# Rounds of four decays, one pool of PSUM banks, and convolution taps that read PSUM, in a fused decoder layer on one core

## The chip, the cores and the metric

The kernel runs on one core of a Trainium2 chip, in fp32 with bf16 and fp16 in places. The metric is the device time of one launch in microseconds. Engines are named as in the profile: PE is TensorE, DVE is VectorE, ACT is ScalarE, POOL is GpSimd, SP is the queue that issues most DMAs.

## What is computed

One decoder layer on 8 batches of 256 tokens of 512 channels: x gains a state-space mixer, then cross-attention to a context, then a mixture of 8 experts (top 2). The change touches the mixer alone. Cut to what matters, per batch:

```
zxbcdt = layernorm(x) @ W_in.T            # z 1024, xBC 1280, dt 64 channels
xBC = silu(causal_conv(xBC, conv_w))      # 4 taps over the tokens, per channel
dt  = softplus(dt_raw + dt_bias);  cum = cumsum(dt * A) within chunks of 128 tokens
L   = exp(cum_i - cum_j) for j <= i       # 64 heads, each 128 x 128 per chunk
Y   = ((C B^T) * L * dt) @ xs  +  exp(cum) * C @ S_prev  +  D * xs
y   = Y * silu(z);  x = x + rmsnorm(y) @ W_out.T
```

## The kernel before

The work is cut into pieces. `mixer_slots` and `attention_slots` give every piece a slot, `whole_order` sorts them, and each engine walks the one list and issues the pieces that are its own; semaphores carry what a piece needs from another engine. So each engine works strictly in this order, and TensorE runs ahead of the others until a semaphore holds it.

The mixer has 256 slots, 32 to a batch, 16 to a chunk, 8 to a unit (a batch, a chunk, half of the heads). A slot s stands for 4 heads and goes through five pieces:

- `decay` (PE, L626): a matmul over 60 rows of bf16 makes the differences of cum for 4 heads, 128x512, in one PSUM bank. Even slots use array rows 0 to 63, odd ones 64 to 127, and two decays are issued together in every even slot.
- `bound` (ACT, L732) takes them out of PSUM into decay, `exp` (ACT, L736) exponentiates in place, two slots after the decay.
- `mix_g` (POOL) for even and `mix_v` (DVE) for odd slots (both L741): the product with C B^T, three slots after, into mix.
- `heads` (PE, L638): for two slots at once, six slots after the decay, 8 products of 32 output columns each (16 records in the trace), into the bank y of the unit.

Around them lie the projections (`x`, `z`, `dt`, L544; each x or z piece has 4 matmuls, 8 records), the turns (L549, L576), the states (L593), the expansion of exp(cum) to channels (`expand`, L598, on 32 rows), the carried part (`carry`, L604), the sum of squares (`ones`, L608) and the output projection (`out`, L616). The table of the expansion is a constant of 64x512, loaded at the start among ten constant loads.

The convolution of a pair of channel tiles: ACT copies the bank of the projection to raw (L690), with three zero columns ahead of it, and once more, scaled with the last tap, to conv (L692, two pieces); DVE adds the other three taps for each of the two tiles (`taps`, L825, 128x256 each, three in a row with a wait between); ACT takes tanh (L700) and DVE gates (L833). The bank is free after ACT's copy.

PSUM has 8 banks. Three (decay_ps) serve decays and later the attention's scores; five (work_ps) serve all the rest. `shared_banks` hands them out in the order of the list: a new piece gets the bank whose last reader stands earliest in the list, and TensorE waits for that reader. Five decay and five mix tiles rotate in SBUF.

Of the kernel before, what the change touches and what calls it, by code (L numbers as in the profile page):

```python
# [40 lines left out]
PAIRS = [4, 0, 1, 2, 3]  # L41
ITEMS = [(kh, par, t, quad) for kh in range(2) for par in range(2) for t in range(TPB) for quad in range(4)]
# [22 lines left out]
class Steps:  # L65
# [5 lines left out]
    def settle(self, instruction):  # L71
        self.n += 1
        instruction.then_inc(self.sem, 1)
        self.e.wait_ge(self.sem, self.n)
# [10 lines left out]
def mixer_slots():  # L85
# [6 lines left out]
    for i in range(NS_STEPS + 6):  # L92
        for s, stage in ((i - 6, "heads"), (i - 3, "mix"), (i - 2, "exp")):
            if 0 <= s < NS_STEPS and (stage != "heads" or s % 2):
                put(i, ((stage + ("_v" if s % 2 else "_g")) if stage == "mix" else stage, s))
        if i < NS_STEPS:
            if i % 2 == 0:
                put(i, ("decay", i), ("decay", i + 1))
            put(i, ("bound", i))

    for u, (b, c, hf) in enumerate(UNITS):
        v = NHALF * u
        if hf == 0:
            put(v - 1, ("cb", b, c))
            put(v, ("cb_mask", b, c))
# [16 lines left out]
        put(f + 12, ("rstat", b, c, hf))  # L122
# [14 lines left out]
    for b in range(NB):  # L137
# [21 lines left out]
        for j, at in zip(PAIRS, (13, 17, 20, 24, 29)):  # L159
# [7 lines left out]
        for j, at in enumerate((32, 36, 39, 43)):  # L167
            put(r + at, ("z", b, j, 0))
            put(r + at + 1, ("z", b, j, 1))
            put(r + at + 2, ("z_tanh", b, j))  # L170
            put(r + at + 3, ("z_gate", b, j))
# [23 lines left out]
def shared_banks(order, size, use):  # L195
# [11 lines left out]
    return bank, opened_after  # L207

# [115 lines left out]
def layer_kernel(nc, A, out):  # L324
# [11 lines left out]
    with ExitStack() as top:  # L336
# [39 lines left out]
        with ExitStack() as st:  # L376
            work_ps = [bank(st, f"work_ps{i}") for i in range(5)]
            decay_ps = [bank(st, f"decay_ps{i}") for i in range(3)]
# [3 lines left out]
            w_in = sb(st, "w_in", [P, KD, 2 * HID + 2 * NS + NH])  # L382
            xnT.append(sb(st, "xnT1", [P, KD, L]))
            raw = [sb(st, f"raw{i}", [P, 2, L + TAPS - 1]) for i in range(2)]
# [1381 lines left out]
```

## Time and profile before

| | us |
|---|---|
| median of 3 runs (1450.73 to 1457.11) | 1454.51 |
| span of the profiled execution (the profile gives no other time of it) | 1459.2 |
| PE busy / DVE / ACT / POOL | 1351.0 / 875.7 / 722.8 / 584.9 |
| PE busy from 700 to 800, 800 to 900, 900 to 1000 us (attention) | 86.9, 83.7, 86.0 |
| PE busy from 1100 to 1459 us (experts) | 348.4 |

The mixer lies between some 51 and 670 us, attention overlaps its end and goes on to about 1000 us, and the experts fill the rest. Busy time counts an engine as busy from the start to the end of its instructions; ends of matmuls are modelled, so that the distance between starts says more than a duration. In a timeline, one line is a run of like instructions: the start, how long the run lasts, and in brackets how long the engine had stood before it and what released it.

### The profile page before, as it was taken

The page shows a single profiled execution, that of the slowest core. Times are in us where ns is not written, and L with a number is a line of the kernel's source. Part 1 is how long each engine was busy: PE and PEld are TensorE (multiplying, and loading weights), DVE is VectorE, ACT ScalarE, POOL GpSimd, SP SyncE. Part 2 cuts the span into 40 slices and gives each one's busy share as a digit, 9 for nine tenths or more (in the row PEclk, how much of TensorE's full clock was granted, in tenths as well). Part 3 has the DMA queues.
Part 4 walks back from the last instruction along what each step waited for, and adds up shares of the span by engine and source line. Part 5 has one row for each costly group of instructions (what it writes and reads, how often), then busy time and mean ns, then how long its engine had stood idle before and what let it go on. Part 6 is the DMA issues. An engine that isn't in the chain of part 4 may idle for free.

```text
span 1459.2 us, 23236 instructions
## 1 busy us (share of the span) xinstructions
PE 1351.0 (93%) x7783; PEld 740.9 (51%) x7783; DVE 875.7 (60%) x1838; ACT 722.8 (50%) x1390; POOL 584.9 (40%) x871
## 2 busy tenths in 40 slices
PE   6799999999999999998888888888999999999997
PEld 4456566566656665654343433324444444444443
DVE  5797888979797879757888898755111111111111
ACT  2677657667667676663587766672111111111110
POOL 1365455555555465674223246143222222222221
PEclk9899999999999999997899999898999999999999
DMA  9000000000000000000211110002343354244322
GB/s 338 10 8 5 8 5 1 12 1 12 1 8 5 8 5 8 13 1 4 98 34 35 34 34 31 30 30 74 119 135 113 70 136 138 45 130 131 58 44 29
DMA packets 40292, 73.02 MB, mean 50 GB/s; under 512 B 18544, under 2 KB 22896, under 8 KB 39152
## 3 DMA queue, kind: packets, MB, share of 16 engines
q1 hardware_dynamic: 30240, 48.10, 9.4%
q0 software_dynamic: 8736, 20.61, 7.7%
q10 hardware_dynamic: 1200, 2.82, 0.5%
q8 instruction: 66, 1.08, 0.3%
q14 instruction: 50, 0.41, 0.1%
HBM read 148.91 MB, written 19.99 MB: 116 GB/s over the span
## 4 chain that ended last, share of the span: by engine, by line
PE 70%; DVE 18%; issue 4%; ACT 3%; POOL 2%; DMA 1%; SPq 1%; POOLq 0%; DVEq 0%; ACTq 0%
PE work_ps L544 13%; PE gate_ps L1540 9%; PE up_ps L1540 9%; PE down_ps L1524 9%; PE work_ps L616 7%; DVE conv L825 6%; PE work_ps L549 4%; PE work_ps L638 3%; DVE maxes L1230 3%; PE work_ps L1056 3%; PE mturn_ps L549 2%; PE decay_ps L626 2%; PE decay_ps L1047 2%; DVE mix L741 1%; PE work_ps L1073 1%
## 5 line engine op out<-in xcount | busy, mean ns | idle before, releaser
L544 PE MATMUL work_ps<-xnT,w_in 128*128 128x256 f32 (+1 forms) x1216 | 303.8, 395 | 0.8 <-ACT xnT L650 0.8
L741 POOL TENSOR_TENSOR mix<-decay,cbm 128x512 f32<-128x512 f32 x128 | 182.0, 1423 | 223.8 <-ACT decay L736 193.4
L544 PEld LDWEIGHTS work_ps<-xnT,w_in 128*128 128x128 f32 (+1 forms) x1216 | 221.8, 190 | 64.3 <-issue 34.0
L732 ACT ACTIVATE decay<-decay_ps 128x512 f32<-128x512 f32 x256 | 154.2, 603 | 117.1 <-PE decay_ps L626 116.4
L1628 POOL DMA_INDIRECT out_dram<-y_out,ids x39 | 61.9, 1587 | 334.5 <-DVE row_w L1592 230.7
L1230 DVE TENSOR_REDUCE maxes<-work_ps 128x2 f32<-128x512 f32 x256 | 166.2, 683 | 32.4 <-PE work_ps L1032 31.1
L825 DVE SCALAR_TENSOR_TENSOR conv<-raw,conv_w,conv 128x256 f32<-128x256 f32 x240 | 179.1, 752 | 7.0 <-ACT conv L692 1.3
L1128 ACT ACTIVATE prob<-decay_ps 128x512 f32<-128x512 f32 x256 | 142.3, 609 | 72.8 <-PE decay_ps L1047 71.9
L1607 DVE TENSOR_TENSOR act<-gelu,up_ps 128x512 f32<-128x512 f32 x39 | 26.8, 688 | 252.1 <-PE up_ps L1540 252.1
L736 ACT ACTIVATE decay<-decay 128x512 f32<-128x512 f32 x256 | 164.1, 641 | 4.6 <-PE work_ps L544 3.0
L1540 PE MATMUL gate_ps<-w_e,xgT 128*128 x312 | 140.5, 593 | 1.4 <-ACT xgT L1557 1.0
L1524 PE MATMUL down_ps<-w_e,actT 128*128 x312 | 140.4, 593 | 0.8 <-ACT actT L1570 0.8
L1540 PE MATMUL up_ps<-w_e,xgT 128*128 x312 | 140.3, 592 | 0.0
L616 PE MATMUL work_ps<-w_out,yz 128*128 128x512 f32 x256 | 132.0, 640 | 4.7 <-DVE yz L883 4.1
L741 DVE TENSOR_TENSOR mix<-decay,cbm 128x512 f32<-128x512 f32 x128 | 100.4, 785 | 35.0 <-PE work_ps L638 19.3
L1599 DVE TENSOR_SCALAR y_out<-down_ps,row_w 128x512 f32<-128x512 f32 x39 | 29.3, 751 | 122.3 <-PE down_ps L1524 122.3
L1032 PE MATMUL work_ps<-kT,qT 48*128 48x256 f16 x512 | 92.4, 295 | 6.5 <-DVE maxes L1230 2.0
L1540 PEld LDWEIGHTS up_ps<-w_e,xgT 128*128 128x128 f32 x312 | 59.3, 190 | 74.6 <-issue 74.6
L1047 PE MATMUL decay_ps<-qT,kT 49*128 49x512 f16 x256 | 90.5, 412 | 6.7 <-ACT prob L1128 5.4
L638 PE MATMUL work_ps<-mix,xdt 128*32 128x128 f32 x2048 | 83.8, 282 | 8.5 <-DVE mix L741 7.7
L1557 ACT ACTIVATE xgT<-mturn_ps 128x512 f32<-128x512 f32 x39 | 23.3, 597 | 136.7 <-PE mturn_ps L549 136.7
L1570 ACT ACTIVATE actT<-mturn_ps 128x512 f32<-128x512 f32 x39 | 23.3, 597 | 128.4 <-PE mturn_ps L549 128.4
(270 smaller groups left out, 1990.0 us busy)
## 6 DMA issues: line engine op xcount, KB each, us to landing
w_e<-c_experts_dram SPq DMA_DIRECT2D x39, 3072.0 KB
normed_tokens<-r_xn SPq DMA_DIRECT2D x17, 256.0 KB, 2.1
out_dram<-x_sb SPq DMA_DIRECT2D x17, 256.0 KB, 2.5
x_sb<-x_dram SPq DMA_DIRECT2D x1, 3072.0 KB, 16.8
w_in<-c_w_inT_dram ACTq DMA_DIRECT2D x1, 2560.0 KB, 12.3
w_in<-c_w_inT_dram SPq DMA_DIRECT2D x1, 2048.0 KB, 9.1
w_out<-c_w_outT_dram SPq DMA_DIRECT2D x1, 2048.0 KB, 22.2
RT<-cum_scratch SPq DMA_DIRECT2D x32, 48.0 KB
```

The costliest lines, as they stand in the source:

```text
L544: m = e.matmul(ps[0:width, at:at + L], w_in[:, k, col:col + width], xnT[b % 2][:, k, :], start=(k == 0), stop=(k == KD - 1))
L616: m = e.matmul(work(stage, tile)[:, :], yz[tile % 2][:, ct, :], w_out[:, ct, :], start=(ct == 0), stop=(ct == NCZ - 1))
L638: m = e.matmul(work("y", b, c, hf)[32 * quad:32 * quad + 32, ct * P:(ct + 1) * P], xdt[hf][:, 2 * HG * ct + h, :], mix[(s - 1 + h // HG) % ...
L732: e.activation(decay[s % 5][:, :], decay_ps[s % 3][:, :], ACT.Relu, scale=-1.0).then_inc(piece_done[stage], 1)
L736: e.activation(decay[s % 5][:, :], decay[s % 5][:, :], ACT.Exp, scale=-1.0).then_inc(piece_done[stage], 1)
L741: return e.tensor_tensor(four(mix[s % 5]), four(decay[s % 5]), cb, ALU.mult)
L825: m = e.scalar_tensor_tensor(o, raw[n % 2][:, i, k:k + L], conv_w[:, c, k:k + 1], o, ALU.mult, ALU.add)
L1047: e.matmul(score_ps[s % 3][:, :], kT[b % 3][base:base + PARTS + 1, k, t * P:(t + 1) * P], qT[b % 3][base:base + PARTS + 1, 2 * k:2 * k + 2 ...
L1128: e.activation(prob[s % 12][:, :], score_ps[s % 3][:, :], ACT.Exp, scale=DH ** -0.5).then_inc(piece_done[stage], 1)
L1230: e.reduce_max(maxes[b % 2][:, t, first:first + 2], work("max", b, p)[:, :].rearrange("p (h t) -> p h t", h=2), AX.X).then_inc(piece_done[ ...
L1524: m = e.matmul(down_ps[i % 2][:, :], actT[i % 2][:, k, :], w_e[:, bass.ds(place[i], 1), k, 2 * EH:].rearrange("p o n -> p (o n)"), start=( ...
L1540: m = e.matmul(ps[:, :], xgT[i % 2][:, k, :], w_e[:, bass.ds(place[i], 1), k, off:off + EH].rearrange("p o n -> p (o n)"), start=(k == 0), ...
```

## The change

- `decay`: four at once, at the head of every fourth slot. `heads` for the two pairs of the round before come directly ahead of them, 8 slots after their own decays. `bound` takes two decays in the first slot of the round and two in the second; `exp` and the products keep their slots.
- The eight banks become one pool, from which mixer pieces take any, attention's pieces the first five, and scores the last three as before. Decays take part in it. Some pieces move by a slot or less, among them `cb`, `cb_mask`, `carry`, `carried`, `rstat`, `z_gate`, and the projections.
- The product is written in place into the decay tile; ten decay tiles replace five decay and five mix tiles.
- The taps read the projection in PSUM; the copy to raw is gone. `taps` is issued as two pieces of three, in which the two tiles alternate. The bank is held until the second of them.
- `dt` (from the second batch), `dt_turn` and `expand` work on all 128 rows and columns: their tiles get 128 partitions, with zeros in the lower half, and the constant of the expansion becomes 128x1024.

```diff
-    for i in range(NS_STEPS + 6):
-        for s, stage in ((i - 6, "heads"), (i - 3, "mix"), (i - 2, "exp")):
-            if 0 <= s < NS_STEPS and (stage != "heads" or s % 2):
-                put(i, ((stage + ("_v" if s % 2 else "_g")) if stage == "mix" else stage, s))
-        if i < NS_STEPS:
-            if i % 2 == 0:
-                put(i, ("decay", i), ("decay", i + 1))
-            put(i, ("bound", i))
+    for i in range(NS_STEPS + 2 * GROUP):
+        if i % GROUP == 0:
+            for s in range(i - 2 * GROUP + 1, i - GROUP, 2):
+                if s >= 0:
+                    put(i, ("heads", s))
+            for s in range(i, min(i + GROUP, NS_STEPS)):
+                put(i, ("decay", s))
+        if 0 <= i - 3 < NS_STEPS:
+            put(i, ("mix_v" if (i - 3) % 2 else "mix_g", i - 3))
+        if 0 <= i - 2 < NS_STEPS:
+            put(i, ("exp", i - 2))
+        for s in range(NS_STEPS):
+            if i == s - s % GROUP + s % GROUP // 2:
+                put(i, ("bound", s))
...
-            put(v - 1, ("cb", b, c))
-            put(v, ("cb_mask", b, c))
+            put(v - 2, ("cb", b, c))
+            put(v - 1, ("cb_mask", b, c))
...
-            put(f + 3, ("carry", b, c, hf))
-            put(f + 5, ("carried", b, c, hf), ("dx_add", b, c, hf))
+            put(f + 2, ("carry", b, c, hf))
+            put(f + 3, ("carried", b, c, hf), ("dx_add", b, c, hf))
...
-        for j, at in zip(PAIRS, (13, 17, 20, 24, 29)):
+        for j, at in zip(PAIRS, (13, 17, 21, 25, 29)):
...
-        for j, at in enumerate((32, 36, 39, 43)):
+        for j, at in enumerate((33, 37, 41, 45)):
...
-        return (stage, *key[:2]), ("x_copy" if stage == "x" else "z_gate", *key[:2])
+        return (stage, *key[:2]), ("taps", *key[:2], 1) if stage == "x" else ("z_gate", *key[:2])
...
+    if stage == "decay":
+        return ("decay", *key), ("bound", *key)
+    if stage == "score":
+        return ("score", *key), ("exponent", *key)
...
-            k = min(range(size), key=lambda i: -1 if last[i] is None else at[last[i]])
+            k = min(allowed(*piece), key=lambda i: -1 if last[i] is None else at[last[i]])
...
+def banks_for(mixer):
+
+    def allowed(stage, *key):
+        if stage == "score":
+            return [5 + key[0] % 3]
+        return range(BANKS if stage in mixer else 5)
+
+    return allowed
...
-            expand = sb(st, "expand", [NH, NCZ // 2, P])
+            expand = sb(st, "expand", [P, NCZ, P])
...
-                channels(e, work(*piece), 0, b, HID + CONV, NH).then_inc(piece_done[stage], 1)
+                channels(e, work(*piece), 0, b, DT_COL, P if b else NH).then_inc(piece_done[stage], 1)
...
-                if s % 2 == 0 and s >= 2:
-                    e.wait_ge(*done("bound", s - 2))
...
-                e.activation(raw[n % 2][:, :, TAPS - 1:TAPS - 1 + L], ps[:, :].rearrange("p (c t) -> p c t", c=2), ACT.Copy)
...
-                if s >= 5:
-                    e.wait_ge(*done(*mixed(s - 5)))
-                e.activation(decay[s % 5][:, :], decay_ps[s % 3][:, :], ACT.Relu, scale=-1.0).then_inc(piece_done[stage], 1)
+                if s >= NDECAY:
+                    e.wait_ge(*done("heads", s - NDECAY + 1 - s % 2))
+                e.activation(decay[s % NDECAY][:, :], work("decay", s)[:, :], ACT.Relu, scale=-1.0).then_inc(piece_done[stage], 1)
...
+        def tap(e, b, j, i, late):
+            o = conv[(5 * b + PAIRS.index(j)) % 2][:, i, late:]
+            return e.scalar_tensor_tensor(o, work("x", b, j)[:, i * L:(i + 1) * L - late], conv_w[:, 2 * j + i, TAPS - 1 - late:TAPS - late], o, ALU.mult, ALU.add)
...
-                for k in range(TAPS - 1):
-                    m = e.scalar_tensor_tensor(o, raw[n % 2][:, i, k:k + L], conv_w[:, c, k:k + 1], o, ALU.mult, ALU.add)
-                    if k < TAPS - 2:
-                        own.settle(m)
-                m.then_inc(piece_done[stage], 1)
+                if part == 0:
+                    e.wait_ge(*done("x_copy", b, j))
+                    first = own.mark(tap(e, b, j, 0, 1))
+                    own.mark(tap(e, b, j, 1, 1))
+                    own.wait(first)
+                    tap(e, b, j, 0, 2).then_inc(piece_done[stage], 1)
+                else:
+                    own.wait(own.n)
+                    second = own.mark(tap(e, b, j, 1, 2))
+                    e.wait_ge(*done("taps", b, j, 0))
+                    own.mark(tap(e, b, j, 0, 3))
+                    own.wait(second)
+                    tap(e, b, j, 1, 3).then_inc(piece_done[stage], 1)
```

## Rows read from the trace of the kernel before

**Rows 1.** Busy time by stretches: start:end, length, busy us of each engine, PEclk, DMA.
```profile
136.00:636.00 500.00, 484.86 (x3420) 310.65 (x3418) 406.47 (x689) 337.77 (x674) 276.21 (x374) 0.99 0.03 6
323.00:350.00 27.00, 24.78 (x192) 16.03 (x191) 26.36 (x40) 18.81 (x40) 13.82 (x12) 1.00 0.05 10
350.00:402.00 52.00, 52.00 (x360) 33.52 (x360) 39.09 (x69) 35.40 (x70) 28.93 (x43) 1.00 0.02 4
...
183.00:189.00 6.00, 6.00 (x20) 4.44 (x21) 5.93 (x8) 2.19 (x6) 3.86 (x4) 0.62 0.01 1
```

**Rows 2.** Chain of waits, 322 to 350 us: start, us, what.
```profile
324.56 1.50 DVE conv L825
...
347.01 0.50 DVE conv L825
```

**Rows 3.** Timeline of TensorE, 335 to 350 us and at 493 us.
```profile
335.41 0.28 PE L576 MATMUL work_ps<-ident,dtT 64*128 64x64 f32 x2
...
336.84 0.39 PE L626 MATMUL decay_ps<-RT,LT 60*128 60x512 bf16 x2 [0.51 <-ACT decay L732]
...
339.79 0.64 PE L638 MATMUL work_ps<-mix,xdt 128*32 128x128 f32 x16 [0.64 <-DVE mix L741]
341.11 1.96 PE L616 MATMUL work_ps<-w_out,yz 128*128 128x512 f32 x4 [0.68 <-DVE yz L883]
...
493.18 0.28 PE L576 MATMUL work_ps<-ident,dtT 64*128 64x64 f32 x2
```

**Rows 4.** Timeline of TensorE, three stretches: starts of neighbouring groups.
```profile
276.67 1.99 PE L544 MATMUL work_ps<-xnT,w_in 128*128 128x256 f32 x8
278.50 0.60 PE L549 MATMUL work_ps<-ident,xn 128*128 128x128 f32 x4
279.03 0.39 PE L626 MATMUL decay_ps<-RT,LT 60*128 60x512 bf16 x2
279.35 1.99 PE L544 MATMUL work_ps<-xnT,w_in 128*128 128x256 f32 x8
281.27 0.64 PE L638 MATMUL work_ps<-mix,xdt 128*32 128x128 f32 x16
...
288.92 0.66 PE L549 MATMUL work_ps<-ident,xbc 128*128 128x128 f32 x4
...
403.97 1.89 PE L544 MATMUL work_ps<-xnT,w_in 128*128 128x256 f32 x8
405.79 0.39 PE L626 MATMUL decay_ps<-RT,LT 60*128 60x512 bf16 x2
```

**Rows 5.** Timeline of TensorE in the attention, 802 us.
```profile
802.16 0.39 PE L1047 MATMUL decay_ps<-qT,kT 49*128 49x512 f16 x1
802.16 0.39 PE L1032 MATMUL work_ps<-kT,qT 48*128 48x256 f16 x2
```

**Rows 6.** Lines of VectorE one by one: durations in ns, least/median/most.
```profile
L825 DVE SCALAR_TENSOR_TENSOR conv<-raw,conv_w,conv x240: 468/485/1560, 29.3 to 608.4; 128x256 f32<-128x256 f32 x120
...
L838 DVE SCALAR_TENSOR_TENSOR zs<-zs,work_ps x32: 665/682/689, 58.2 to 636.5; 128x512 f32<-128x512 f32 x32
...
L865 DVE TENSOR_TENSOR xdt<-work_ps,dt_tok x64: 403/410/425, 57.0 to 659.1; 128x256 f32<-128x256 f32 x64
...
L883 DVE TENSOR_TENSOR yz<-yz,zs x32: 691/693/1049, 80.5 to 685.3; 128x512 f32<-128x512 f32 x32
...
L900 DVE SCALAR_TENSOR_TENSOR x_sb<-work_ps,rstats,x_sb x16: 735/745/752, 118.4 to 703.4; 128x512 f32<-128x512 f32 x16
```

**Rows 7.** Busy time by stretches, line L825 alone.
```profile
323.00:350.00 27.00, 14.81 (x18) 1.00 0.05 10
```

**Rows 8.** Timeline of ScalarE in the first batch.
```profile
44.35 0.58 ACT L690 ACTIVATE raw<-work_ps 128x512 f32<-128x512 f32 x1
```

**Rows 9.** DMA issues: count, size, median us to landing.
```profile
xbc<-c_select_dram SPq DMA_DIRECT2D x1, 512.0 KB, 4.7
...
expand<-c_expand_dram SPq DMA_DIRECT2D x1, 128.0 KB, 4.3
```

More of the change, by code:

```diff
@@ L121, in mixer_slots @@
         put(f + 11, ("ones", b, c, hf))
-        put(f + 12, ("rstat", b, c, hf))
+        put(f + 11.5, ("rstat", b, c, hf))
         if hf == 1:
@@ L170, in mixer_slots @@
             put(r + at + 2, ("z_tanh", b, j))
-            put(r + at + 3, ("z_gate", b, j))
+            put(r + at + 2.9, ("z_gate", b, j))
     return slots
@@ L376, in layer_kernel @@
         with ExitStack() as st:
-            work_ps = [bank(st, f"work_ps{i}") for i in range(5)]
-            decay_ps = [bank(st, f"decay_ps{i}") for i in range(3)]
+            work_ps = [bank(st, f"work_ps{i}") for i in range(BANKS)]
             w_out = sb(st, "w_out", [P, NCZ, DIM])
@@ L381, in layer_kernel @@
             xw = sb(st, "xw", [P, NH, HP])
-            w_in = sb(st, "w_in", [P, KD, 2 * HID + 2 * NS + NH])
+            w_in = sb(st, "w_in", [P, KD, X_COL + CONV])
             xnT.append(sb(st, "xnT1", [P, KD, L]))
-            raw = [sb(st, f"raw{i}", [P, 2, L + TAPS - 1]) for i in range(2)]
             conv = [sb(st, f"conv{i}", [P, 2, L]) for i in range(2)]
@@ L404, in layer_kernel @@
             wdec_tok = [sb(st, f"wdec_tok{i}", [P, NH]) for i in range(2)]
-            ecum = [sb(st, f"ecum{i}", [NH, P]) for i in range(2)]
+            ecum = [sb(st, f"ecum{i}", [P, P]) for i in range(2)]
             LT = sb(st, "LT", [P, TPB, NG // 2, P], BF16)
@@ L411, in layer_kernel @@
             state = sb(st, "state", [P, HID])
-            decay = [sb(st, f"decay{i}", [P, HG * P]) for i in range(5)]
-            mix = [sb(st, f"mix{i}", [P, HG * P]) for i in range(5)]
+            decay = [sb(st, f"decay{i}", [P, HG * P]) for i in range(NDECAY)]
             eexp = sb(st, "eexp", [P, 512])
@@ L568, in tensor_mixer @@
                     e.wait_ge(load_w["xbc" if stage == "x" else "z"], 16)
-                col = (HID if stage == "x" else 0) + (2 * j + half) * P
+                col = (X_COL if stage == "x" else 0) + (2 * j + half) * P
                 channels(e, work(stage, b, j), half * L, b, col, P).then_inc(piece_done[stage], 1)
@@ L597, in tensor_mixer @@
                 for k in range(4):
-                    m = e.matmul(work(*piece)[:, k * P:(k + 1) * P], expand[heads_of(hf), k, :], ecum[b % 2][heads_of(hf), :], start=True, stop=True)
+                    m = e.matmul(work(*piece)[:, k * P:(k + 1) * P], expand[:, 4 * hf + k, :], ecum[b % 2][:, :], start=True, stop=True)
                 m.then_inc(piece_done[stage], 1)
@@ L622, in tensor_mixer @@
                     e.wait_ge(load_cum[c], 16 * 8 * (b + 1))
-                if s % 2 == 0 and s >= 2:
-                    e.wait_ge(*done("bound", s - 2))
                 rows = slice(64 * (s % 2), 64 * (s % 2) + DROWS)
-                e.matmul(decay_ps[s % 3][:, :], LT[rows, c, (hf * NHALF + s % NHALF) // 2, :], RT[rows, c, :], start=True, stop=True).then_inc(piece_done[stage], 1)
+                e.matmul(work(*piece)[:, :], LT[rows, c, (hf * NHALF + s % NHALF) // 2, :], RT[rows, c, :], start=True, stop=True).then_inc(piece_done[stage], 1)
             elif stage == "heads":
@@ L638, in tensor_mixer @@
                         m = e.matmul(work("y", b, c, hf)[32 * quad:32 * quad + 32, ct * P:(ct + 1) * P], xdt[hf][:, 2 * HG * ct + h, :],
-                                     mix[(s - 1 + h // HG) % 5][:, h % HG * P:(h % HG + 1) * P], start=(odd == 0), stop=(odd == 1), tile_position=(0, 32 * quad))
+                                     decay[(s - 1 + h // HG) % NDECAY][:, h % HG * P:(h % HG + 1) * P], start=(odd == 0), stop=(odd == 1), tile_position=(0, 32 * quad))
                 m.then_inc(piece_done[stage], 1)
@@ L740, in mixing @@
             four = lambda a: a[:, :].rearrange("p (h i) -> p h i", h=HG)
-            return e.tensor_tensor(four(mix[s % 5]), four(decay[s % 5]), cb, ALU.mult)
+            return e.tensor_tensor(four(decay[s % NDECAY]), four(decay[s % NDECAY]), cb, ALU.mult)
+        def tap(e, b, j, i, late):
+            o = conv[(5 * b + PAIRS.index(j)) % 2][:, i, late:]
+            return e.scalar_tensor_tensor(o, work("x", b, j)[:, i * L:(i + 1) * L - late], conv_w[:, 2 * j + i, TAPS - 1 - late:TAPS - late], o, ALU.mult, ALU.add)
         def vector_mixer(e, own, piece):
@@ L767, in vector_mixer @@
                 for i in range(2):
-                    e.memset(raw[i][:, :, 0:TAPS - 1], 0.0)
                     e.memset(xdt[i][:, :, :], 0.0)
+                    e.memset(ecum[i][NH:, :], 0.0)
+                e.memset(dtT_all[NH:, 5, :], 0.0)
+                e.memset(wdecT_all[NH:, :], 0.0)
                 e.wait_ge(load_ident, 16)
```

55 lines of the change are left out of this document (29 added, 26 removed).

## The prediction

> **What bounds the kernel now.** The change touches only the mixer, some 51 to 670 us, so I began with the busy time by stretches [rows 1]. Over 136 to 636 us TensorE is busy 484.9 of 500 us, VectorE 406.5, ScalarE 337.8, GpSimd 276.2. Batches repeat: the decay turn at 335.41 comes again at 493.18, two batches on [rows 3], so one batch takes 78.9 us. Inside one batch there are two regimes [rows 1]. From 350 to 402 TensorE is busy for all 52 us and VectorE for 39.1. From 323 to 350 VectorE is busy 26.4 of 27 us and TensorE 24.8. The chain of waits, read next, agrees: its links from 324.56 to 347.01 are nearly all VectorE's, mostly the convolution's taps (L825) [rows 2], and TensorE's timeline shows it standing for 0.51, 0.64 and 0.68 us there, for a decay's reader, a product and yz [rows 3]. So TensorE and VectorE each decide in a part; ScalarE and GpSimd do not.
>
> **TensorE's busy time is not all work.** It runs in modes: full array, heads on 32 columns (L638), decays on 64 rows (L626), the expansion on 32 rows. Starts of neighbouring groups give what a change of mode costs [rows 4]. The same eight L544 matmuls take 1.83 us with heads before and full work behind (276.67 to 278.50), 1.82 with full work before and decays behind (403.97 to 405.79), and 1.92 with decays before and heads behind (279.35 to 281.27). So a change behind a group costs 1.92 - 1.83 = 0.09 us, and a full group that follows a tiled one is 1.92 - 1.82 = 0.10 longer. The second differs by group: four L549 take 0.66 after decays and 0.60 after full work, 0.06 more. Over the mix of groups I take 0.07; 0 and 0.10 are its bounds.
>
> **The change, part by part.**
>
> 1. Rounds of four. Now every two slots have one run of heads and one of decays, in different slots: 128 runs each, 512 changes in or out. 39 neighbouring pairs save one each; the expansion and the two dt stages bring it to 504 in the written order, 224 of them into full work. With the rounds the order is full, heads, decays, full once in four slots: 64 x 3 = 192, and 3 for the first batch's dt: 195, 66 of them into full work. The later dt, dt_turn and expand become full work. Gone: (504 - 195) x 0.093 = 28.7 us, and (224 - 66) x 0.07 = 11.1: together 39.8 us, 5.0 us a batch (bounds 28.7 and 44.5). It is all on the path where TensorE decides.
> Four decays in a row don't occur in the trace. If the second pair's weights could not be loaded beneath the first, each round would lose 0.09: 5.8 us. The nearest rows are in the same 64-row mode: two L1032 of one row group with 256 columns each take 0.39 us, and so does one L1047 with 512 [rows 5], which leaves nothing for weights. I take 0; the 5.8 stays in the range.
> The Trainium skill, "TensorE: Matmul & The Clock Gate", Part 3, The mechanism, lets a weight load pass under a running matmul only where the row group differs. By it the gain would be those 5.8 us smaller; the rows speak against it.
>
> 2. The taps. There are 240, at least 468 ns, 485 in the median, 1560 at most [rows 6]. Another operation that reads two SBUF tiles stretches as well (L883, 691 to 1049), while those with an operand in PSUM don't: L838 665 to 689, L865 403 to 425, L900 735 to 752 [rows 6]. So I put the stretching down to GpSimd at work on SBUF beside it, and it should go with the operand. The tap will read PSUM and one SBUF tile and take a scalar per partition, as L900 does: 745 ns for 512 columns, less 682 - 410 = 272 for half the columns (L838, L865): 473, and I take 480. Bounds: 410, and what it costs now. In the VectorE stretch lie 18 taps with 14.8 us [rows 7], 823 ns each: 18 x 0.48 = 8.6, so 6.2 us go. There VectorE would need 26.4 - 6.2 = 20.2 us, and TensorE 24.8 - 27/79 x 5.0 = 23.1. TensorE becomes the bound there too. The 27 - 24.8 = 2.2 us of standing go in each of 8 batches: 17.6 us.
> The Trainium skill, "VectorE: DVE Perf Modes", The TRN2 errata, gives an operation that reads PSUM 62 cycles more than one from SBUF, some 65 ns as an estimate from it. Here the least of L883 (SBUF) is 691 and the median of L838 (PSUM) 682 [rows 6], so no such term. By the page a tap would be dearer by it: 1.2 us in a VectorE stretch, 9.4 us in all if VectorE still decided there, none if not.
>
> 3. ScalarE loses the copy to raw: 40 x 0.58 = 23 us [rows 8], off the path in the steady part. The product in place (L741) costs what it did.
>
> 4. New waits. Eight banks are shared, and a round takes four at once. By the order, seven of a batch's 32 decays get a bank whose reader stands only one slot ahead (x_add, yz, xdt, carried), and the heads of slot 4g+3 have two slots after their product in place of three. TensorE is in order, so behind a waiting decay stands everything, the projections that feed VectorE too. In the TensorE stretch VectorE has 12.9 of 52 us free; in the other it would have 23.1 - 20.2 = 2.9. I take 1 us of new standing a batch: +8 us; bounds 0 and 3 a batch, the upper one a little over what stands today.
>
> 5. Start. The first batch's chain of convolution pairs runs through ScalarE's copy to raw; 44.35 is the last of three [rows 8]: -1.7 us. The expansion table grows from 128 to 512 KB, ahead of the last constants: 128 KB landed in 4.3 us, the 512 KB of select in 4.7 [rows 9]: +0.4, and under 2. Four new memsets of at most 256 columns cost under the 0.41 of L865 each: +0.6, between 0 and 1.6.
>
> 6. dt_turn moves 128 columns for 64; an L549 of 128 columns is some 0.11 us (0.53 from 278.50 to 279.03, less 0.09, by four) [rows 4], so 3 x 0.05 x 8 = 1.2 us. dt with 128 output columns streams the same 256. No DMA is added beyond the table; SP's cum_in waits for the 16th decay of a half, now issued two slots earlier, and nothing else passes it.
>
> Sum: -39.8 - 17.6 + 8 - 1.7 + 0.4 + 0.6 + 1.2 = -48.9 us on the profiled execution's span of 1459.2, the only time that the profile gives for it. The span is 4.7 us above the median of 1454.5, so I take the difference off the median: 1405.6, or 1405. Attention and the experts (from 700 us) should not move.
>
> **The rivals.**
>
> A. The waits that leave also give back clock. From 183 to 189 us the granted clock is 0.62 [rows 1], the lower level of 1.2 GHz for some three quarters of it, though TensorE is busy throughout; those 6 us hold the work of 3.7, so 2.3 are lost. If no new waits come (-8) and two such places go (-5): 1392. For: VectorE has 2.9 us spare. Against: shorter leads, and that the clock over the whole stretch is 0.99, so such places are few.
>
> B. The short leads bite in VectorE's stretch: three rounds lie there and each stands 1 us, 16 us over the sum: 1421. For: VectorE's chain is unbroken for 23 us there. Against: 6 us are taken from it.
>
> C. The taps don't become short, since what stretches them is not the second SBUF operand but the tile they write. VectorE then needs its 26.4 us as now, the stretch stays at 27 us, and only 52/79 of the 39.8 comes: -26, and +1 for the start: 1430. Against: the PSUM rows [rows 6]. It is also the case in which the change of the convolution does not do what it says.
>
> D. Slower: the round as a lockstep. Each of 64 rounds begins with heads that need the last product, and its fourth decay needs a bank just read; ScalarE gets four decays at once and none between, and TensorE stands in each round until ScalarE and VectorE have caught up. It decides from 48.9/64 = 0.76 us a round on. At 1.0 us, one and a half of VectorE's operations (0.68), it gives +15: 1469. Against: in 52 of 79 us VectorE is 75% busy, and a round has some 9 us of other matmuls.
>
> **How the numbers follow.** Forecast 0.52, A 0.15, B 0.19, C 0.07, D 0.07. The likeliest is 1405, its own range 1392 to 1418. From A's 1392 the upper bound of part 1 (-5) and an easier start (-4) lead to 1383; above, C ends at 1430, and D is left out. A difference within 0.5% (7.3 us) is what a measurement of this kernel can't tell from none. Slower by more: D, 0.06; same: 0.03, D's milder end and what lies between C and it; faster: the rest, 0.91.
>
> **What would show it.** L638 and the decays together in the timeline, once in four slots. A batch of 72 to 74 us. Taps of 450 to 500 ns without spread (part 2); over 550 is C. TensorE busy over 97% in the former VectorE stretch; standing in front of decays or heads there is B, in every round D. From the first of four decays to the full group behind them 0.55 us (part 1); 0.64 means that the second pair's weights are not hidden. The forecast is wrong if the batch comes out above 76 us, or if the stages from 700 us on change their length.

## The result, and the profile after

| | before | after |
|---|---|---|
| median | 1452.74 us (1450.73 to 1457.11) | 1394.91 us (1394.34 to 1402.02) |
| span of the profiled execution | 1459.2 | 1392.4 |
| one batch, decay turn to decay turn | 78.88 | 71.46 |
| TensorE standing in that batch | 2.22 | 1.00 |

The ratio is 0.960, with an interval of 0.957 to 0.963: 57.8 us less, where 48.9 were forecast. A decay turn is the turn of dt, once a batch (`dt_turn`); the batch is the same in both, from the fifth such turn to the sixth (335.41 to 414.29 [rows 3], and 301.11 to 372.57). Standing is all time in which no matmul runs, gaps too short for the lists of waits included; the rest of a batch is called TensorE's own time. Lines have moved: the projections are L572, heads L664, decays L652, the output projection L644, the taps L771, the product L767, yz L918 and L920.

The page of the changed kernel; its first line of busy time answers to the table of before.

```profile
span 1392.4 us, 23244 instructions
PE 1286.9 (92%) x7783; PEld 739.6 (53%) x7783; DVE 822.8 (59%) x1840; ACT 705.9 (51%) x1350; POOL 580.8 (42%) x871
PEclk9999999999999999987999999989999999999999
```

TensorE is busy for 64 us less and VectorE for 53. Now the stretches that answer to [rows 1] (start:end, length, busy us of each engine, granted clock, DMA share, GB/s): the whole steady part, the stretch in which VectorE used to decide (it lies from 12.4 us ahead of the decay turn to 14.6 behind it, here 289 to 316), and the stretch behind it.

```profile
136.00:560.00 424.00, 414.75 (x3240) 296.16 (x3238) 348.67 (x667) 302.99 (x603) 257.30 (x348) 0.99 0.03 7
289.00:316.00 27.00, 26.20 (x210) 19.16 (x209) 23.49 (x47) 19.95 (x43) 15.64 (x13) 1.00 0.05 10
316.00:360.00 44.00, 43.80 (x339) 30.84 (x338) 33.88 (x62) 32.13 (x62) 27.36 (x42) 1.00 0.02 5
```

In the former VectorE stretch VectorE is busy for 23.5 of 27 us where it was for 26.4, and TensorE for 97% of it. So TensorE is now the busier of the two in both parts, though VectorE has only 3.5 us to spare in this one. TensorE's timeline there and a little behind it, answering to [rows 3, 4]:

```profile
301.11 0.38 PE L604 MATMUL work_ps<-ident,dtT 128*128 128x128 f32 x2
...
303.26 0.65 PE L664 MATMUL work_ps<-decay,xdt 128*32 128x128 f32 x16
304.56 0.64 PE L664 MATMUL work_ps<-decay,xdt 128*32 128x128 f32 x16 [0.65 <-DVE decay L767]
305.13 0.61 PE L652 MATMUL work_ps<-RT,LT 60*128 60x512 bf16 x4
305.88 1.96 PE L644 MATMUL work_ps<-w_out,yz 128*128 128x512 f32 x4
307.67 1.05 PE L626 MATMUL work_ps<-ecum,expand 128*128 128x128 f32 x8
308.56 1.89 PE L572 MATMUL work_ps<-xnT,w_in 128*128 128x256 f32 x8
...
317.10 1.08 PE L664 MATMUL work_ps<-decay,xdt 128*32 128x128 f32 x32
318.11 0.61 PE L652 MATMUL work_ps<-RT,LT 60*128 60x512 bf16 x4
318.65 1.55 PE L644 MATMUL work_ps<-w_out,yz 128*128 128x512 f32 x3
```

A round is one run of heads (1.01 us from start to start, 32 records) and one of decays (0.54), then full work. The expansion's eight matmuls take 0.89 from start to start, now on the full array. The one longer wait is for VectorE's product, with heads behind it. VectorE is still on the path there: in the chain of waits (start, us, what) it holds from 292.1 to 305.8 us, nearly 14 us where it was 23 [rows 2], and TensorE stands for 0.80 us by its end:

```profile
287.73 3.47 PE work_ps L572 x16
...
292.10 1.26 DVE conv L771 x3
...
299.65 1.62 DVE decay L767
...
301.47 1.63 DVE conv L771 x5
...
303.81 0.60 DVE decay L767
304.41 0.61 DVE yz L918
...
305.04 0.70 DVE yz L920
...
305.88 1.96 PE work_ps L644 x4
```

The taps and the product one by one (least/median/most in ns), answering to [rows 6]:

```profile
L771 DVE SCALAR_TENSOR_TENSOR conv<-work_ps,conv_w,conv x240: 459/469/484, 30.6 to 549.8; 128x255 f32<-128x255 f32 x40, 128x254 f32<-128x254 f32 x40, 128x253 f32<-128x253 f32 x40
L767 DVE TENSOR_TENSOR decay<-decay,cbm x128: 629/691/1817, 52.4 to 617.9; 128x512 f32<-128x512 f32 x128
```

No tap is stretched any more. The product on VectorE still is, and more often: its mean is 966 ns, 785 before.

**Where the time came from.** By the starts of the decay turns, the mixer's last heads end at 682.0 before and 621.1 after, 60.9 us earlier. The start gives 1.4, and the eight batches, counted from turn to turn and the last one to its end, 6.3, 8.2, 10.4, 8.1, 7.4, 7.4, 1.5 and 10.3. The seventh gives only 1.5: it takes 77.4 us. There TensorE stands before heads again, and in this execution the granted clock falls right behind. TensorE's waits from 444 to 522 us (engine, line, released by: us, times, longest), and the stretch after the longest:

```profile
PE work_ps L664 <- DVE decay L767: 2.7, 2, 2.1
PE work_ps L572 <- DVE xdt L902: 0.6, 1, 0.6
```

```profile
515.00:522.00 7.00, 5.66 (x31) 3.85 (x32) 6.86 (x23) 5.24 (x12) 4.32 (x10) 0.60 0.08 18
```

Ahead of that product VectorE works through the first pieces of attention (three of L1239, 0.6 us each, between 507 and 515) beside the decays' sums and the taps. A granted clock of 0.60 is the lower level of 1.2 GHz for four fifths of the 7 us, 2.8 us lost. The wait cost 2.1 and the clock behind it more. The fall does not always come: in the run with 4 us of delay (below) the same heads wait 2.07 us, the 7 us behind have a clock of 1.00, and the seventh batch takes 75.7 us.

The rest of the profiled difference lies in attention, whose code is unchanged. From its first score to its last, and on to the experts; before:

```profile
704.00:981.00 277.00, 239.12 (x1865) 104.19 (x1865) 228.40 (x611) 199.22 (x376) 103.19 (x264) 0.92 0.13 43
981.00:1028.00 47.00, 38.95 (x169) 19.20 (x166) 22.32 (x100) 10.02 (x17) 13.01 (x13) 0.85 0.18 57
```

after:

```profile
644.00:916.00 272.00, 231.91 (x1868) 102.14 (x1868) 228.47 (x614) 199.35 (x376) 103.14 (x264) 0.97 0.13 44
916.00:961.00 45.00, 36.19 (x161) 17.36 (x161) 21.29 (x98) 9.73 (x16) 12.94 (x13) 0.89 0.19 60
```

The other engines are busy as long as before to 0.2 us; TensorE's granted clock is 0.97 and not 0.92. The experts take 431.7 and 431.4 us.

### The profile page after: what moved, and what is told of

Same layout as the page of the kernel before. It is cut to its first block, busy times and chain, and to the rows that moved or that the text cites. A ratio compares the mean times of both kernels' runs of the same rounds, so it can differ in the third digit from the quotient of the medians.

```text
span 1392.4 us, 23244 instructions
## 1 busy us (share of the span) xinstructions
PE 1286.9 (92%) x7783; PEld 739.6 (53%) x7783; DVE 822.8 (59%) x1840; ACT 705.9 (51%) x1350; POOL 580.8 (42%) x871
## 4 chain that ended last, share of the span: by engine, by line
PE 66%; DVE 18%; issue 6%; ACT 5%; POOL 3%; DMA 1%; SPq 1%; POOLq 0%; DVEq 0%; ACTq 0%
PE work_ps L572 12%; PE gate_ps L1573 10%; PE up_ps L1573 10%; PE down_ps L1557 9%; PE work_ps L644 7%; PE work_ps L577 4%; DVE maxes L1263 3%; DVE conv L771 3%; PE work_ps L1089 3%; PE mturn_ps L577 2%; DVE decay L767 2%; PE work_ps L664 2%; PE work_ps L1080 2%; ACT prob L1161 1%; PE work_ps L652 1%
## 5 line engine op out<-in xcount | busy, mean ns | idle before, releaser
L572 PE MATMUL work_ps<-xnT,w_in 128*128 128x256 f32 (+1 forms) x1216 | 289.1, 386 | 4.3 <-DVE xdt L902 2.4
L572 PEld LDWEIGHTS work_ps<-xnT,w_in 128*128 128x128 f32 (+1 forms) x1216 | 226.8, 193 | 54.8 <-issue 21.9
L767 POOL TENSOR_TENSOR decay<-decay,cbm 128x512 f32<-128x512 f32 x128 | 183.8, 1437 | 147.4 <-ACT decay L762 144.3
L1161 ACT ACTIVATE prob<-work_ps 128x512 f32<-128x512 f32 x256 | 142.3, 609 | 66.2 <-PE work_ps L1080 65.6
L758 ACT ACTIVATE decay<-work_ps 128x512 f32<-128x512 f32 x256 | 138.7, 600 | 38.4 <-PE work_ps L652 37.8
L767 DVE TENSOR_TENSOR decay<-decay,cbm 128x512 f32<-128x512 f32 x128 | 123.6, 966 | 25.3 <-ACT decay L762 25.3
L644 PE MATMUL work_ps<-w_out,yz 128*128 128x512 f32 x256 | 127.9, 623 | 1.8 <-DVE yz L920 1.0
L771 DVE SCALAR_TENSOR_TENSOR conv<-work_ps,conv_w,conv 128x255 f32<-128x255 f32 (+2 forms) x240 | 97.5, 469 | 1.3 <-ACT conv L718 1.1
L1065 PE MATMUL work_ps<-kT,qT 48*128 48x256 f16 x512 | 88.3, 282 | 10.0 <-ACT qT L1155 3.5
L1080 PE MATMUL work_ps<-qT,kT 49*128 49x512 f16 x256 | 87.7, 392 | 7.5 <-ACT prob L1161 6.2
L1573 PEld LDWEIGHTS gate_ps<-w_e,xgT 128*128 128x128 f32 x312 | 56.2, 190 | 58.1 <-issue 58.1
```

The lines of the kernel that those rows point to most:

```text
L572: m = e.matmul(ps[0:width, at:at + L], w_in[:, k, col:col + width], xnT[b % 2][:, k, :], start=(k == 0), stop=(k == KD - 1))
L644: m = e.matmul(work(stage, tile)[:, :], yz[tile % 2][:, ct, :], w_out[:, ct, :], start=(ct == 0), stop=(ct == NCZ - 1))
L758: e.activation(decay[s % NDECAY][:, :], work("decay", s)[:, :], ACT.Relu, scale=-1.0).then_inc(piece_done[stage], 1)
L767: return e.tensor_tensor(four(decay[s % NDECAY]), four(decay[s % NDECAY]), cb, ALU.mult)
L771: return e.scalar_tensor_tensor(o, work("x", b, j)[:, i * L:(i + 1) * L - late], conv_w[:, 2 * j + i, TAPS - 1 - late:TAPS - late], o, ALU ...
L1065: m = e.matmul(work(*piece)[:, hh * L:(hh + 1) * L], qT[b % 3][base:base + PARTS, 2 * k + hh, t * P:(t + 1) * P], kT[b % 3][base:base + PA ...
```

## The experiments

Each ran beside the kernel before on the same chip. Besides the time I read the steady batch (decay turn to decay turn), what TensorE stands in it, and attention from first to last score, since the last moves by itself (below).

**The taps alone.** The kernel before, with the changed taps and without the copy; everything else as it was.

```diff
+        def tap(e, b, j, i, late):
+            o = conv[(5 * b + PAIRS.index(j)) % 2][:, i, late:]
+            return e.scalar_tensor_tensor(o, work("x", b, j)[:, i * L:(i + 1) * L - late], ...
...
-                e.activation(raw[n % 2][:, :, TAPS - 1:TAPS - 1 + L], ...
```

> The kernel before with the convolution alone changed: taps read the projection in PSUM, no copy to raw, the two tiles alternate, the bank is held until the last tap; five and three banks, pairs of decays and all modes as before. Theory (VectorE decides some 27 us of each batch, and the taps stretch because of their second SBUF operand): taps 450 to 500 ns without spread, the standing of TensorE of 2.2 us a batch nearly gone, -17.6 - 1.7 us: 1433 us, batch 76.7 us. Rival (TensorE decides everywhere, the standing comes from the short lead of its order, not from VectorE's load): taps short all the same, but 1449 to 1452 us. Rival (the stretch comes with the tile that is written): taps at 700 ns or more in the mean, 1450 us.

Measured: 1424.81 us (1423.06 to 1429.74), ratio 0.981 (0.978 to 0.983): 29.9 us less, and 8 us below the theory's 1433. The batch is 76.42, 2.46 less than 78.88. A whole batch by engines:

```profile
244.00:321.00 77.00, 77.00 (x561) 49.85 (x562) 60.04 (x110) 52.13 (x104) 42.31 (x55) 1.00 0.03 7
```

TensorE does not stand at all. So it was the stretched taps that made VectorE the bound in the kernel before, and what the short ones give a batch is TensorE's former standing, as part 2 said. The other 10 us are outside the steady batch: the stretch behind the seventh batch is 9.2 us shorter (granted clock 0.94 over it, before 0.89), and the second and third batches 3.5 and 5.3 us.

**The rounds alone.** The changed kernel, with the copy to raw and the taps from raw; the bank is free after the copy.

```diff
-            o = conv[(5 * b + PAIRS.index(j)) % 2][:, i, late:]
-            return e.scalar_tensor_tensor(o, work("x", b, j)[:, i * L:(i + 1) * L - late], ...
+            n, k = 5 * b + PAIRS.index(j), TAPS - 1 - late
+            o = conv[n % 2][:, i, :]
+            return e.scalar_tensor_tensor(o, raw[n % 2][:, i, k:k + L], ...
```

> The changed kernel with the taps' operand undone: ScalarE copies to raw again, the taps read raw in SBUF (in the new alternating order), the bank is free after the copy; rounds, pool and full arrays stay. Theory: the taps stretch again to some 780 ns, VectorE's stretch stays at 26 to 27 us, and the rounds pay only in the other part of the batch: 52/79 of some 50 us, 1420 us, 25 above the changed kernel. Rival (the two parts add): the changed kernel plus what the taps gave alone, some 19 us: 1414 us. Rival (rounds carry all): 1397 us.

Measured: 1433.27 us (1429.46 to 1440.43), ratio 0.985 (0.983 to 0.987): 21.4 us less. The third to the sixth batch take 74.5, 74.1, 74.2 and 77.1 us, 74.96 on the mean. Taps, and a stretch in the place of the former VectorE stretch:

```profile
L774 DVE SCALAR_TENSOR_TENSOR conv<-raw,conv_w,conv x240: 462/474/1516, 32.0 to 584.9; 128x256 f32<-128x256 f32 x120
```

```profile
310.00:337.00 27.00, 24.90 (x197) 17.55 (x197) 26.69 (x45) 20.61 (x44) 20.91 (x14) 1.00 0.05 10
```

The taps stretch again, VectorE is full, and TensorE stands 2.8 us a batch, 1.5 of it for the product ahead of heads. All three times of the expectation were too fast. In the batch the two parts alone give 2.46 + 3.92 = 6.38 us, together 7.42; in the medians 29.9 + 21.4 = 51.3 against 57.8, but that difference is no larger than what attention moves by itself. By the batch, shorter matmuls are worth their full size only where VectorE can follow.

**The copy kept.** The changed kernel, with ScalarE's copy to a tile that nobody reads.

```diff
+                e.activation(raw[n % 2][:, :, TAPS - 1:TAPS - 1 + L], ps[:, :].rearrange("p (c t) -> p c t", c=2), ACT.Copy)
```

> The changed kernel with ScalarE's copy to raw put back, though nothing reads it. Theory (the copy is off the path in the steady part and on it only in the first batch): +1.7 us, 1396 to 1397 us. Rival (ScalarE's queue feeds tanh, exp and so the products, and the copy delays them): up to 40 x 0.6 = 24 us more, 1410 to 1419 us.

Measured: 1405.85 us (1399.65 to 1409.43), ratio 0.966 (0.963 to 0.968). The batch is 71.92, 0.46 more than 71.46, and TensorE's waits of one batch say where:

```profile
PE work_ps L665 <- DVE decay L769: 1.1, 1, 1.1
PE work_ps L622 <- ACT dtT L690: 0.2, 1, 0.2
```

The heads stand 1.1 for 0.65. In the order the taps wait for ScalarE's piece, which is now longer, and VectorE's product stands behind the taps; that this is the way the delay takes is my reading, no run isolates it. In the profile the mixer ends 2.1 us later; the rest of the difference is attention at 279.3 us with a clock of 0.92. So "off the path" was wrong, by some 2 us in the profile and 3.7 by eight times the batch.

**Rounds of two.** The changed kernel, with heads and two decays in every second slot, and one `bound` in each slot.

```diff
-        if i % GROUP == 0:
-            for s in range(i - 2 * GROUP + 1, i - GROUP, 2):
-                if s >= 0:
-                    put(i, ("heads", s))
-            for s in range(i, min(i + GROUP, NS_STEPS)):
-                put(i, ("decay", s))
+        if i % 2 == 0:
+            if 0 <= i - 5 < NS_STEPS:
+                put(i, ("heads", i - 5))
+            if i < NS_STEPS:
+                put(i, ("decay", i), ("decay", i + 1))
```

> The changed kernel with rounds of two: in every even slot one run of heads and directly behind it two decays (full, heads, decays, full), pool, in-place product, taps and full arrays as changed, the same least lead of two slots from product to heads. Changes of mode: 3 x 128 + 3 = 387 in place of 195, into full work 130 in place of 66. Theory (a change of mode costs 0.093 us, an entry into full work 0.07 to 0.11 more): +17.9 + 4.5 to 7 = +22 to +25 us, 1417 to 1420 us. Rival (the gain comes from the pool of banks and the order, not from the modes): within 5 us of the changed kernel, 1390 to 1400 us.

Measured: 1414.07 us (1409.46 to 1416.95), ratio 0.972 (0.970 to 0.974). The steady batch is 74.30, 2.85 more. TensorE:

```profile
319.69 0.64 PE L662 MATMUL work_ps<-decay,xdt 128*32 128x128 f32 x16
320.26 0.39 PE L650 MATMUL work_ps<-RT,LT 60*128 60x512 bf16 x2
320.58 1.98 PE L642 MATMUL work_ps<-w_out,yz 128*128 128x512 f32 x4
```

Two such rounds take 2 x (0.57 + 0.32) = 1.78 us to the full group, one round of four 1.01 + 0.54 = 1.55. TensorE stands 0.85 us in this batch and 1.00 in the changed kernel's, so its own time is 2.98 longer, with the same matmuls. A batch has 24 changes of mode more, 2.2 us at 0.093; the 0.75 left are 0.09 for each of the 8 further entries into full work. In the batch, then, the loss is not one of waiting. Over the whole kernel it is smaller than eight times 2.85, or 22.8: attention took 271.6 us in both, and the profile is 16.1 us longer, since the first batch loses only 1.6 and the last is 2.4 us shorter than in the changed kernel, with a clock of 0.965 for 0.940. The medians lie 19.2 apart where the theory had 22 to 25; the rival's 1400 is excluded.

**Changes of mode added.** In every round two matmuls of the full array with one column each, once both ahead of the round's heads (next to full work, no change more), once behind each pair of heads (three changes more in a round: out of heads, in again, and out again).

```diff
+                e.matmul(work("decay", key[0])[:, 0:1], ident[:, :], ones[:, 0:1], start=True, stop=True)
```

> The changed kernel with two small full-array matmuls of one column added to each of the 64 rounds, both ahead of the heads, in full mode: the control for extra_between, modes unchanged. Such a matmul (two records) took 0.115 to 0.14 us in the sum of squares (L636): +15 to +18 us, 1410 to 1413 us. Their results are overwritten, the output is the same.

> The same two matmuls, one between the two runs of heads and one between heads and decays: three more changes of mode a round and two more entries into full work. Theory (0.093 a change, 0.1 an entry when weights can't be loaded ahead): 62 rounds x 0.48 = +30 us over extra_ahead, about 1440 us, on TensorE's starts as well as in the time. Rival (the price belongs to the large groups behind a change and a short matmul does not pay it): +18 us at most, 1430. Rival (modes cost nothing, only the order did): as extra_ahead, 1411.

Measured: ahead 1413.14 us (1405.79 to 1418.84), ratio 0.969 (0.966 to 0.972), batch 73.00; between 1436.95 us (1434.23 to 1438.72), ratio 0.986 (0.983 to 0.989), batch 76.04. The same matmuls in the same number; the timeline of TensorE, first ahead, then between:

```profile
311.41 0.50 PE L606 MATMUL work_ps<-ones,ident 128*128 128x1 f32 x4
311.85 1.08 PE L672 MATMUL work_ps<-decay,xdt 128*32 128x128 f32 x32
312.86 0.60 PE L660 MATMUL work_ps<-RT,LT 60*128 60x512 bf16 x4
313.39 1.13 PE L652 MATMUL work_ps<-w_out,yz 128*128 128x512 f32 x2
```

```profile
318.80 0.64 PE L672 MATMUL work_ps<-decay,xdt 128*32 128x128 f32 x16
319.38 0.38 PE L606 MATMUL work_ps<-ones,ident 128*128 128x1 f32 x2
319.69 0.65 PE L672 MATMUL work_ps<-decay,xdt 128*32 128x128 f32 x16
320.26 0.38 PE L606 MATMUL work_ps<-ones,ident 128*128 128x1 f32 x2
320.58 0.61 PE L660 MATMUL work_ps<-RT,LT 60*128 60x512 bf16 x4
321.11 1.13 PE L652 MATMUL work_ps<-w_out,yz 128*128 128x512 f32 x2
```

From the first line shown to the full group it is 1.98 us ahead and 2.31 between. Over a batch with no standing in either kernel it is 3.04 us in 8 rounds, 0.38 a round: three changes at 0.093, which leaves 0.05 for each of the two short entries (the theory had 0.48 a round and 1440 us). The medians are 23.8 us apart for matmuls whose work did not change, with no wait involved: a change of mode has a price of its own, and it is on the path. How it comes about stays open. The weight load of the added matmul starts 0.21 us ahead of it in full work (311.20, the matmul at 311.41) and 0.01 ahead behind heads (319.37 and 319.38), so that a part of the price can be a load that no longer hides; no run separates it from the change itself.

**Part of the array again.** The changed kernel, with dt, dt_turn and expand back on part of the array.

```diff
-                e.matmul(..., expand[:, 4 * hf + k, :], ecum[b % 2][:, :]
+                e.matmul(..., expand[heads_of(hf), 4 * hf + k, :], ecum[b % 2][heads_of(hf), :]
```

> The changed kernel with dt (64 columns), dt_turn (64 rows) and expand (32 rows) back on part of the array; rounds, pool, taps as changed, the larger table is still loaded. Four places a batch then leave full work and come back. Theory (0.19 us for the two changes and 0.05 to 0.10 for the entry, less 0.1 for the shorter turn): batch 71.45 + 4 x 0.27 - 0.1 = 72.4 us, +8 us, 1403 us, give or take the 3 us of one execution's attention. Rival (TensorE stands 0.9 us a batch anyway and the places fall where it has slack): batch 71.5 to 71.8 us, 1396 to 1399 us.

Measured: 1408.32 us (1402.55 to 1411.33), ratio 0.968 (0.965 to 0.971). The batch is 72.56, 1.10 more. Without its standing (0.79 and 1.00) TensorE needs 1.31 more; priced as in part 1, the eight changes and four entries of a batch are 1.02, less 0.15 for the wider dt_turn. The rival, that the places fall where TensorE has slack, is excluded.

**Order inside the round.** Two tries for a faster kernel: decays ahead of heads, so that the heads have longer for their product; and the round's last product one slot earlier (its exponential half a slot), which is what TensorE waits for.

```diff
-            put(i, ("mix_v" if (i - 3) % 2 else "mix_g", i - 3))
+            early = (i - 3) % GROUP == GROUP - 1
+            put(i - early, ("mix_v" if (i - 3) % 2 else "mix_g", i - 3))
```

> The changed kernel with the four decays ahead of the two runs of heads in each round; as many changes of mode. Theory (TensorE stands 0.5 to 0.65 us a batch at the second run of heads for VectorE's product; the decays, 0.54 us, now pass ahead of it): standing there nearly gone, -0.5 x 8 = -4 us, 1391 us. Rival (the decays then wait for their banks in place of the heads, and y is given another bank): no change or up to 5 us slower.

> The changed kernel with the last product of each round one slot earlier in VectorE's order (and its exp half a slot earlier in ScalarE's), so that the second run of heads has three slots behind its product again. Theory (TensorE stands 0.65 us a batch there): batch 70.9 in place of 71.45 us, -4 us: 1391 us, if the attention keeps its 271.6 us; up to 1399 if it does not. Rival (ScalarE and VectorE then serve something else later): batch 71.4 us or more.

Measured: decays first 1408.06 us (1407.64 to 1410.96), ratio 0.966 (0.964 to 0.969), batch 72.32; product early 1427.46 us (1423.52 to 1430.16), ratio 0.981 (0.977 to 0.984), batch 74.57. Both theories fell. Decays first stands as long as the changed kernel (1.09 us, now 0.68 for yz) and is slower by 0.8 a batch in TensorE's own time. Of that 0.7 lies in the decays: of a batch's eight runs of four, two take 0.92 and 0.95 us from start to start and the others 0.54. A wait for a bank that is shorter than the decay still running would look like this; the rows don't say that it is one. With the product early TensorE stands 3.37 us a batch. Its waits from 300 to 450 us:

```profile
PE work_ps L653 <- DVE xdt L903: 3.0, 2, 1.5
PE work_ps L645 <- DVE yz L921: 2.0, 2, 1.0
PE work_ps L665 <- DVE decay L768: 1.1, 2, 0.5
```

VectorE is in order too: it now waits for the exponential (10.0 us a batch, 2.2 in the changed kernel) ahead of xdt and yz, and these hold decay banks and the output projection. The heads still wait 0.5.

**What moves attention.** The theory was that the place where attention starts in time decides its clock. Two kernels stand 2 and 4 us at the start of VectorE (memsets of a tile that nothing uses yet), one is the changed kernel itself once more.

```diff
+                for i in range(4):
+                    own.settle(e.memset(squares[:, :], 0.0))
```

> The changed kernel, not edited, a second time: does the length of its attention (271.6 us, granted clock 0.97) belong to the kernel or to the execution? If to the kernel: 1392 to 1397 us and attention 271 to 272 us again, if to the execution: attention anywhere from 271 to 280 us, with times spread up to 1402.

> The changed kernel with four memsets of 512 columns added to VectorE's constants, which lie on the chain of the start: mixer and attention are the same instructions, some 2 us later. Theory (the granted clock in the unchanged attention depends on where it comes to lie in time; of nine kernels so far two have 271.6 us at 0.97 and the others 274 to 281 us at 0.91 to 0.93): the attention may come out at 277 to 280 us: 1397 + 6 to 8 = 1403 to 1405 us. Rival (what the others lost comes from their edits): attention 271.6 us, 1397 us.

> As delay_2us with eight memsets, some 4 us later. Theory: attention of another length than in delay_2us or the changed kernel, 271 to 281 us, so 1399 to 1408 us, not in proportion to the delay. Rival: attention 271.6 us, 1399 us.

Measured: the changed kernel 1400.21 us (1397.39 to 1403.87), ratio 0.962 (0.959 to 0.966); with 2 us 1403.57 (1395.62 to 1404.79), ratio 0.964 (0.961 to 0.968); with 4 us 1407.33 (1402.80 to 1412.22), ratio 0.968 (0.964 to 0.971). Attention of the changed kernel in this second profile:

```profile
641.00:918.00 277.00, 239.41 (x1867) 103.80 (x1864) 228.29 (x615) 199.44 (x376) 103.53 (x264) 0.93 0.13 43
```

and with 2 us of delay:

```profile
646.00:917.00 271.00, 231.23 (x1863) 101.67 (x1861) 227.53 (x611) 199.35 (x376) 103.12 (x264) 0.97 0.13 44
```

The same kernel has attention of 271.6 us at 0.97 in one execution and of 277.0 at 0.93 in the other; a delay of 2 us gives 271.6 again, one of 4 us 275.6 at 0.95. So a difference of this size comes about between executions of one kernel and can't be put down to a change. What decides it stays open, and with one profile of each kernel the place in time is not excluded as a part of it. The medians with a delay are 3.4 and 7.1 us above the changed kernel's, with intervals that overlap for the first. The changed kernel's own two medians, 1394.91 and 1400.21, lie 5.3 us apart.

None of these kernels is faster than the changed one.

## Why the prediction came out right

**Part 1, the modes: right in kind, too small.** Without its standing, TensorE needs 70.46 us a batch for 76.66: 6.20 less, where the modes less the wider dt_turn had 5.0 - 0.15 = 4.85. By the experiments, in TensorE's own time: from rounds of two to four 2.98 (by the terms 24 x 0.093 + 8 x 0.07 = 2.79); dt, dt_turn and expand 1.31 (0.87). The remaining 1.91, where the terms have 1.2, is heads and decays made neighbours, with the pool of banks and its small shifts; no run isolates it. So both terms are borne out as a sum, and a little small; the runs don't separate them. With 0.093 for a change, rounds of two give 0.09 for an entry in place of 0.07. The counts were a little small too: in the trace a steady batch has 64 changes before and 24 after, 29 and 8 of them into full work, so 40 and 21 fewer where the forecast had 38.6 and 19.8. And the expansion's own group shrank from 1.08 us, start to start, to 0.89, 0.10 more than the one change behind it, twice a batch; the prediction had no term for that. These three are about 0.9 us; the rest of the 1.35 by which part 1 is short stays open. Over eight batches it is 11 us, nearly the whole distance of 12.0 between the forecast and the 60.9 us that the mixer gained in the profiles.

**Four decays in a row** take 0.54 us (forecast 0.55; 0.64 if the second pair's weights were not hidden), and 0.22 more than two [rows 4]. The rule of the Trainium skill that the prediction set against the rows, in "TensorE: Matmul & The Clock Gate", Part 3, The mechanism, that a weight load overlaps a running matmul only where the row group differs, would have it 0.09 longer; the trace has no such time.

**Part 2, the taps: right.** 469 ns without spread (forecast 480), and -2.46 us a batch alone (2.2). A tap that reads PSUM is no dearer than an undisturbed one from SBUF (469 against 474 ns in the medians of the changed kernel and of the rounds alone). Two readings of SBUF beside GpSimd stretch an operation, one of PSUM does not: 240 taps have a most of 484 ns from PSUM, of 1516 from SBUF in the same order of work. The kernel before shows it tap by tap: those with no work of GpSimd beside them take 483 ns on the mean, the 137 with over 0.3 us of it 954; in the changed kernel the 178 with over 0.3 us take 469. The Trainium skill says as much in "SBUF — State Buffer", Who interferes with whom: a VectorE instruction with two SBUF inputs contends with a GpSimd instruction that reads SBUF. The taps agree with it, and so does the product: in the 46 that took over 900 ns a product of GpSimd ran beside them for 0.80 us on the mean, in the other 82 for 0.12.

**Part 3, the copy: "off the path" was wrong**, by 0.46 us a batch. So was "the product in place costs what it did": VectorE's product takes 966 ns on the mean for 785, some 2.9 us of VectorE a batch (an estimate from 16 products), and it is the product that TensorE's longest wait is for.

**Part 4, new waits: right on the mean, wrong in its evenness.** 1 us a batch was taken. A steady batch has 1.00: 0.65 before heads for the product, 0.20 for a bank with dt in it, 0.14 for yz. No decay stands. But the seventh batch stands 4.0 us and loses clock, some 6 us against the others, and this is a wait like rival B's at one place, though outside the stretch that B names; attention's first pieces lie on VectorE's chain ahead of it, which the prediction did not look at.

**The start** came 1.4 us earlier (0.7 forecast). **Attention and the experts** "should not move": the experts did not; attention did, by 5.5 us in the profiles, and by its own condition the prediction counts this against itself. It moves between executions of one kernel as much.

**The rivals.** A took part: the second to the fourth batch and the last gave more than a steady one does; over the last the clock is 0.94 for 0.89, which by (1 - clock) x length is 6.0 us lost for 12.0, and the third had 0.96 before and 1.00 after, 3.4 us. But its condition, no new waits, is not met. That the result, 1394.9, lies nearer to A's 1392 than to the forecast's 1405 comes mostly from part 1's size. B did not come in its stretch, where TensorE stands 0.80 us and not 3 a batch. C is excluded by the taps, D by a steady batch that stands once in eight rounds.

**The sum.** 8 x 7.42 = 59.4 us if all batches were as the fifth; 1.1 less in the first, 4.4 more in the second to the fourth, 6.0 less in the seventh, 2.9 more in the last, and 1.4 from the start: 61.0 from rounded terms, and the mixer of the profile ends 60.9 earlier. The forecast had 48.9 for all of it; part 1 is short by 11. The batch of 71.46 lies below the 72 to 74 that the prediction named, for the same reason. That the gains of clock in single batches and the loss in the seventh nearly cancel is luck.

## What to carry to other kernels

Put matmuls that use the array in the same way next to each other, and count changes: here each cost 0.09 us behind the group that leaves and 0.05 to 0.10 in the group that enters full work, which no wait and no busy share shows, only the distance between starts. Look for what the second engine has left before you shorten the first; here the halves alone gave 2.5 and 3.9 us a batch and both gave 7.4, since VectorE's stretched taps ate a part of what the rounds save. Before two profiles are compared by stretches, lay the stretches by the same event in both, here the decay turn. Compare variants in a repeated stretch of the trace, not by their total alone, when another stage has a clock of its own.

## What the hardware showed beyond the forecast

- Attention, unchanged, took from 271.6 us (clock 0.97) to 280.4 (0.91) in fourteen profiled executions, and 271.6 and 277.0 in two of the same kernel. Differences of under 9 us between two kernels in this document rest on the batch, not on the total.
- VectorE's product became slower (785 to 966 ns on the mean) though its operands are the same and it only writes in place. It lies beside GpSimd's product for 0.36 us and not 0.15 us on the mean of 128. The kernel with the taps alone writes into another tile as before and has 888 ns with 0.30 us of overlap, so the overlap goes with it and writing in place is not needed for it. This is read from traces, not isolated.
- The same wait of 2.1 us on TensorE in the seventh batch was followed by a granted clock of 0.60 over 7 us in one execution and of 1.00 in the run with 4 us of delay; the waits of 0.65 in steady batches were followed by 1.00. So the length of a wait alone does not decide whether the clock falls. In the kernel before it was 0.62 from 183 to 189 us with TensorE busy throughout [rows 1].
